# Seven of sixteen layer-0 products as three rounded matmuls, three chunks per tile scaled in PSUM, and another order in the last group

## The chip, the cores and the metric

The kernel runs on one core of one Trainium2 chip. The metric is the device time of one execution in microseconds (us), as a median over runs. Everything is float32, so TensorE works either on float32 operands or on operands rounded to its rounded type (float32r), of which several are needed for one float32 product.

## What is computed

The reference is three layers of a compressed interaction network. Each layer forms, for every batch row and embedding element, all products of a field of the current features with a field of the input, multiplies them by a weight matrix and sums over the embedding.

```python
# input: (512, 64, 16); W0: (128, 64*64); W1, W2: (128, 64*128); b: (128,)
x_vec = input
for W, b in params:
    z = jnp.einsum('bhd,bfd->bhfd', x_vec, input)
    z = z.reshape(B, h * f, d)
    x_vec = jnp.einsum('oc,bcd->bod', W, z) + b[None, :, None]
    outs.append(x_vec.sum(axis=2))
return jnp.concatenate(outs, axis=1)          # (512, 384)
```

## The kernel before

**Tiles and groups.** A column is one (batch row, embedding element) pair. 128 columns (8 batch rows) are a tile, four tiles are a group, and 16 groups cover the batch. TensorE works through the groups one after the other (`groups`, bodies "first", 14 times "inner", "last"), each body in 64 steps `e`: four tiles `j` of 16 chunks `c`, so `e = 16 j + c`.

**Layer 1** is the bulk. A step computes one chunk: `y` (128 columns x 512) by `by_parts` (line 686), which is three rounded matmuls, xh by wh, xh by wl and xl by wh, where h is the rounded upper part of an operand and l the remainder. Four PSUM banks hold chunks, so chunk c+4 waits until chunk c has been read. A chunk holds four fields. Each must be scaled by its column's field value in `x0t` and added up. VectorE does that for 11 of 16 chunks with four instructions each (`add_fields`, lines 617 and 619). ScalarE scales the five HELPED chunks (1, 4, 7, 10, 13) into `prod` (`multiply`, line 525), and GpSimd adds these (lines 369, 371). `combine` on GpSimd (lines 377 to 382) then makes the tile's `x2`.

**Layer 0 of the next group** is made between the chunks. SyncE copies shifted rows of the input `xg` into one of nine slots of `z` (`front`, line 296, two transfers per step `t`), GpSimd multiplies the slot by `xg` (`product`, line 360), and TensorE multiplies by `w0t` in float32 (`layer0`, line 705) at the steps `AHEAD_AT` (9, 11, 14, ... 55 for t = 0 ... 16). A slot is loaded again once its matmul has read it (`z_used`). The last step, t = 16, is one rounded matmul (line 701). In the first group the rest of group 0's own layer 0 (384 columns) runs in steps 0 to 11 (`LATER_AT`), and only then does group 1's begin.

**Layer 2** needs `x2` of the tile before (line 767, at c = 12), and once in four groups, and at the end, 64 float32 matmuls (line 755, `quarter`). In steps 12 to 27 of the first group the 16 pieces of W2 are transposed (line 744) and copied out by ScalarE (`w2_out`, line 482).

**Order.** Every engine runs its own hand-written list in order, with semaphores between. Nothing reorders it. The turn of a group (steps 56 to 63 and 0 to 8) holds no layer-0 matmul, but ScalarE and VectorE split the new layer-0 result there (`upper`, line 463; `fields`, line 450; `lower`, line 594; `sum_elements`, line 601). `own_rows` (line 584) is VectorE's other work, once per tile.

**Before and after the groups.** The prologue pairs and transposes W0 (line 803), computes layer 0 of the first 128 columns in float32 (`early_layer0`, line 727, 16 matmuls) and splits W1 (lines 544 and 673). After the last chunk come `combine` on GpSimd, layer 2 of the last tile, the last quarter, 12 transposes (line 860), four copies and four stores.

## Time and profile before

| what | us |
|---|---|
| three runs | 1128.06, 1128.33, 1129.62 |
| median | 1128.33 |
| the profiled execution's own time | 1127.95 |
| its span, first to last instruction | 1126.2 |
| TensorE busy | 1095.7 (97%) |
| VectorE busy | 868.8 (77%) |
| GpSimd busy | 836.8 (74%) |
| ScalarE busy | 451.4 (40%) |
| mean granted TensorE clock | 0.997 of full |

The profiled execution took 1.75 us more than its span, which lies before and after the instructions, and 0.38 us less than the median. A matmul's end in the trace is modelled and matmuls overlap, so a group's busy time says little of what one costs. What one costs is read from the distance between starts, or from the chain of waits, which counts only the time to the next step. A float32 matmul stands as two records, so "x2" at line 705 is one matmul.

### The profile page before, as it was taken

To read this page: it belongs to the slowest core of one execution; us is meant where nothing else is said; L and a number is where in the kernel's file an instruction comes from. 1 tells how busy PE (TensorE), PEld (TensorE's weight loads), DVE (VectorE), ACT (ScalarE), POOL (GpSimd) and SP (SyncE) were. 2 spreads that over 40 slices of the span, in tenths; PEclk is the share of its full clock that TensorE was granted. 3 is DMA by queue.
4 is the path that set the end of the run, shared out by engine and by line. 5 is a ranking of instruction groups with operands and counts; after the bars stand their busy time and mean duration, and the time that the engine had idled before them with its cause. 6 is when DMAs were issued, how large, how long until landed. Compare 5 with 4: busy or idle time off the path is not lost.

```text
span 1126.2 us, 17047 instructions
## 1 busy us (share of the span) xinstructions
PE 1095.7 (97%) x4690; PEld 786.3 (70%) x4690; DVE 868.8 (77%) x3008; ACT 451.4 (40%) x1533; POOL 836.8 (74%) x765
## 2 busy tenths in 40 slices
PE   5989999999999999999999999999999999999996
PEld 5766667666677667666678666676677776666776
DVE  3556879888884888879794798978887598888990
ACT  1443435343432444434351343534343243434550
POOL 4568887969784697878875788787978479697561
PEclk9999999999999999999999999999999999999998
DMA  7952414223141231405141051423323142240000
GB/s 245 251 114 60 112 54 94 73 56 104 17 122 36 58 102 24 124 27 122 46 103 47 17 122 45 105 62 80 87 42 95 31 94 73 51 109 9 1 1 29
DMA packets 112352, 85.82 MB, mean 76 GB/s; under 512 B 75136, under 2 KB 77920, under 8 KB 112128
## 3 DMA queue, kind: packets, MB, share of 16 engines
q1 hardware_dynamic: 110528, 78.37, 28.9%
q10 hardware_dynamic: 1728, 6.36, 1.5%
q8 instruction: 37, 0.61, 0.2%
q14 instruction: 59, 0.48, 0.1%
HBM read 14.75 MB, written 0.79 MB: 14 GB/s over the span
## 4 chain that ended last, share of the span: by engine, by line
PE 83%; DVE 13%; issue 2%; DMA 1%; ACT 1%; POOL 1%; SPq 0%; POOLq 0%; ACTq 0%
PE y L692 53%; PE l L705 19%; DVE acc L619 8%; PE xt L755 5%; PE l2p L767 3%; DVE bd L584 2%; DVE w1l L673 1%; DVE x1l L594 1%; DMA gram<-in_L_rec_W_dram 1%; PE l2p L744 1%; DMA z<-xg 0%; PE l2p L717 0%; ACT prod L525 0%; PE xt L737 0%; PE l L727 0%
## 5 line engine op out<-in xcount | busy, mean ns | idle before, releaser
L619 DVE SCALAR_TENSOR_TENSOR acc<-y,x0t,acc 128x128 f32<-128x128 f32 x2560 | 698.8, 341 | 206.1 <-PE y L692 204.0
L525 ACT ACTIVATE prod<-y,x0t 128x128 f32<-128x128 f32 x1280 | 366.0, 369 | 610.5 <-PE y L692 578.7
L692 PE MATMUL y<-w1h,x1h 128*128 128x512 f32 x1024 | 509.3, 497 | 6.0 <-DVE acc L619 4.3
L692 PE MATMUL y<-w1h,x1l 128*128 128x512 f32 x1024 | 403.5, 394 | 0.0
L692 PE MATMUL y<-w1l,x1h 128*128 128x512 f32 x1024 | 402.4, 393 | 0.0
L371 POOL TENSOR_TENSOR pacc<-pacc,prod 128x512 f32<-128x512 f32 x192 | 247.4, 1289 | 191.6 <-ACT prod L525 191.6
L360 POOL TENSOR_TENSOR z<-z,xg 128x512 f32<-128x512 f32 (+2 forms) x272 | 348.3, 1288 | 23.7 <-DMA z<-xg 23.7
L692 PEld LDWEIGHTS y<-w1h,x1h 128*128 128x128 f32 x1024 | 192.8, 188 | 132.8 <-issue 59.2
L705 PE MATMUL l<-z,w0t 128*128 128x512 f32 (+1 forms) x512 | 257.5, 585 | 0.6 <-POOL z L360 0.6
L692 PEld LDWEIGHTS y<-w1l,x1h 128*128 128x128 f32 x1024 | 192.8, 188 | 82.2 <-issue 54.1
L692 PEld LDWEIGHTS y<-w1h,x1l 128*128 128x128 f32 x1024 | 192.1, 188 | 43.6
L705 PEld LDWEIGHTS l<-z,w0t 128*128 128x128 f32 x512 | 95.5, 189 | 23.7 <-POOL z L360 1.9
L369 POOL TENSOR_TENSOR pacc<-prod 128x512 f32<-128x512 f32 x64 | 85.4, 1334 | 28.7 <-ACT prod L525 28.7
L377 POOL TENSOR_TENSOR pacc<-pacc,acc 128x512 f32<-128x512 f32 x64 | 83.1, 1298 | 4.0 <-DVE acc L619 3.3
L755 PEld LDWEIGHTS xt<-gram,w2t 128*128 128x128 f32 x512 | 63.0, 197 | 3.6 <-ACT sums L470 1.5
L755 PE MATMUL xt<-gram,w2t 128*128 128x128 f32 x512 | 63.4, 281 | 0.8 <-ACT sums L470 0.8
L584 DVE TENSOR_TENSOR bd<-x0t,own_half 128x256 f32<-128x256 f32 x64 | 62.4, 976 | 0.0
L617 DVE TENSOR_SCALAR acc<-y,x0t 128x128 f32<-128x128 f32 x192 | 54.9, 341 | 0.0
L379 POOL TENSOR_TENSOR pacc<-pacc 128x256 f32<-128x256 f32 x64 | 46.9, 732 | 5.0
L767 PE MATMUL l2p<-bd,x 64*128 64x260 f32 x256 | 45.9, 435 | 4.5 <-POOL x L382 4.5
L468 ACT COPY gram<-l2p 128x512 f32<-128x512 f32 x64 | 38.6, 603 | 5.5 <-PE l2p L767 5.5
L767 PEld LDWEIGHTS l2p<-bd,x 64*128 64x128 f32 x256 | 19.5, 186 | 27.9 <-issue 22.5
(65 smaller groups left out, 300.8 us busy)
## 6 DMA issues: line engine op xcount, KB each, us to landing
z<-xg SPq DMA_DIRECT2D x480, 128.0 KB, 2.4
xg<-in_r_input_dram SPq DMA_DIRECT2D x32, 128.0 KB, 3.9
w2t<-in_L_rec_W_dram ACTq DMA_DIRECT2D x8, 512.0 KB, 7.1
gram<-in_L_rec_W_dram SPq DMA_DIRECT2D x8, 512.0 KB, 5.9
z<-xg SPq DMA_DIRECT2D x32, 96.0 KB, 4.0
z<-xg SPq DMA_DIRECT2D x15, 192.0 KB
gram<-in_L_rec_W_dram ACTq DMA_DIRECT2D x1, 2048.0 KB, 7.9
out_dram<-z SPq DMA_DIRECT2D x4, 192.0 KB, 2.1
```

What stands on the lines that cost most here:

```text
L360: nc.gpsimd.tensor_tensor(z[0:rows, slot, cols], z[0:rows, slot, cols], xg[0:rows, cols], ALU.mult).then_inc(z_made, 1)
L369: nc.gpsimd.tensor_tensor(pacc[:], prod[:, 0], prod[:, 1], ALU.add).then_inc(pool_step, 1)
L371: nc.gpsimd.tensor_tensor(pacc[:], pacc[:], prod[:, h % HSLOTS], ALU.add).then_inc(pool_step, 1)
L377: nc.gpsimd.tensor_tensor(pacc[:], pacc[:], acc[:, slot], ALU.add).then_inc(pool_step, 1)
L525: last = nc.scalar.activation(prod[:, h % HSLOTS, k, :], y[c % YB][:, k * O:(k + 1) * O], ACT.Copy, scale=x0t[:, j, f:f + 1])
L584: nc.vector.tensor_tensor(bd[:, j % 2, 0:GRAM].rearrange("p (b f) -> p b f", f=F), x0t[:, j, :].unsqueeze(1).to_broadcast(shape), own_half ...
L617: ins = nc.vector.tensor_scalar(to, of, x0t[:, j, f:f + 1], None, ALU.mult)
L619: ins = nc.vector.scalar_tensor_tensor(out=to, in0=of, scalar=x0t[:, j, f:f + 1], in1=b1r[:] if m == 0 else to, op0=ALU.mult, op1=ALU.add)
L692: ins = nc.tensor.matmul(to, stationary, moving, start=(first and k == 0), stop=(last and k == 2))
L705: nc.tensor.matmul(l0[:, cols], w0t[:, t, :], z[:, slot, cols], start=(t == 0), stop=False).then_inc(z_used, 1)
L755: last = nc.tensor.matmul(l2, w2t[:, f, :], gram[:, f, :], start=(f == 0), stop=(f == F - 1))
L767: last = nc.tensor.matmul(l2p[:, k, 0:GRAM + HALF_B], x2[half, slot], bd[half, slot, :], start=True, stop=True)
```

## The change

- `PARTED` is the seven odd steps t = 1, 3, ... 13 of layer 0. Their products are split by ScalarE (`part_upper`, a rounding copy of `z` into `zh`) and VectorE (`part_lower`, `z` minus `zh` into `zl`), and TensorE uses `by_parts` on them with split weights `w0h` and `w0l`. Nine steps stay float32. Two slots hold `zh` and `zl`. In the prologue, W0 is split in the same way, and `early_layer0` does each parted step with two float32 matmuls instead of one.
- To make room, `z` has six slots instead of nine. In the first group GpSimd makes 6 products ahead instead of 9. In the others one product moves from step 0 of tile 3 to step 4 of tile 2.
- Chunks 3, 9 and 15 of each tile (3, 9 and 12 in the last group) are scaled in place in PSUM by ScalarE (`scale`, four instructions), and VectorE adds the whole chunk to `acc` with one instruction instead of four.
- In the last group, the first three of four output rows are transposed and copied during the chunks. At the end VectorE combines the last tile in two instructions instead of GpSimd in three. One output row is left for the end.

```diff
-ZSLOTS = 9
+ZSLOTS = 6
+PARTED = tuple(range(1, 15, 2))
+ZHSLOTS = 2
+SCALED = (3, 9, 15)
+SCALED_LAST = (3, 9, 12)
+ROWS_AT = (34, 40, 46)
-LATER_PRODUCTS = (9, (2, 2, 2, 2, 0))
-AHEAD_FIRST_AT = [22 + t * 33 // (ZT - 1) for t in range(ZT)]
+LATER_PRODUCTS = (6, (3, 3, 3, 2, 0))
+AHEAD_FIRST_AT = [24 + t * 31 // (ZT - 1) for t in range(ZT)]
+LATER_PARTED_AT = [{t: LATER_AT[t] - k for t in PARTED} for k in (2, 1)]
+PARTED_AT = [{AHEAD_AT[t] - k: t for t in PARTED} for k in (6, 4)]
-PRODUCTS_AT = ((2, 1, 1, 1, 1), (1, 1, 1, 1, 1), (1, 1, 1, 1, 0), (2, 0, 0, 0, 0))
+PRODUCTS_AT = ((2, 1, 1, 1, 1), (1, 1, 1, 1, 1), (1, 1, 1, 1, 1), (1, 0, 0, 0, 0))
...
+            def part_upper(n, t):
...
+                act.wait_ge(z_made, ZT * n + t + 1)
...
+                nc.scalar.copy(zh[:, i % ZHSLOTS, cols], z[:, zslot(t), cols]).then_inc(zh_made, 1)
...
+            def scale(tile, j, c):
+
+                act.wait_ge(y_made, CHUNKS * tile + c + 1)
+                for k in range(CF):
+                    f = CF * c + k
+                    of = y[c % YB][:, k * O:(k + 1) * O]
+                    last = nc.scalar.activation(of, of, ACT.Copy, scale=x0t[:, j, f:f + 1])
+                last.then_inc(y_scaled, 1)
...
+            def part_lower(n, t):
...
+                dve.wait_ge(zh_made, i + 1)
+                nc.vector.tensor_tensor(zl[:, i % ZHSLOTS, cols], z[:, zslot(t), cols],
+                                        zh[:, i % ZHSLOTS, cols].bitcast(F32), ALU.subtract).then_inc(zl_made, 1)
...
+                if c in scaled_in(tile):
+                    dve.wait_ge(y_scaled, scaled_at(tile, c))
+                    dve.wait_ge(acc_step, added(tile, SUMMED[m - 1]))
+                    to = acc[:, j % 2].rearrange("p k o -> p (k o)")
+                    nc.vector.tensor_tensor(to, y[c % YB][:], to, ALU.add).then_inc(acc_step, 1)
+                    return
...
+                if t in PARTED:
+                    i = PARTED.index(t)
+                    at = (PN * n + i) % ZHSLOTS
+                    pe.wait_ge(zl_made, PN * n + i + 1)
+                    by_parts(l0[:, cols], zh[:, at, cols], zl[:, at, cols], w0h[:, i, :], w0l[:, i, :],
+                             t == 0, False, False).then_inc(z_used, 1)
+                    return
```

The order on **TensorE** at steps 29 to 32 of an inner group. The rows are chunks (`y`) and a layer-0 product into `l`. Before:

```order
L692 MATMUL y<-w1h,x1l 128x512
L705 MATMUL l<-z,w0t 128x512
L692 MATMUL y<-w1h,x1h 128x512
L692 MATMUL y<-w1l,x1h 128x512
L692 MATMUL y<-w1h,x1l 128x512
```

and now:

```order
L817 MATMUL y<-w1h,x1l 128x512
L817 MATMUL l<-zh,w0h 128x512
L817 MATMUL l<-zh,w0l 128x512
L817 MATMUL l<-zl,w0h 128x512
L817 MATMUL y<-w1h,x1h 128x512
```

One float32 matmul has become three rounded ones at the same place.

The order on **ScalarE** at the turn of a group, from the split of the new layer 0 (`x1h`, 384 columns) to the late `x0t`. The rows between are `prod`, the copies of layer 2 and the split of the last 128 columns. Before:

```order
L463 ACTIVATE x1h<-l,b0c 128x384
L450 COPY x0t<-xt 128x192
L525 ACTIVATE prod<-y,x0t 128x128 x8
L468 COPY gram<-l2p 128x64x8
L470 COPY sums<-l2p 128x8
L463 ACTIVATE x1h<-l,b0c 128x128
L525 ACTIVATE prod<-y,x0t 128x128 x8
L450 COPY x0t<-xt 128x64
```

and now:

```order
L527 ACTIVATE x1h<-l,b0c 128x384
L514 COPY x0t<-xt 128x192
L604 ACTIVATE y<-y,x0t 128x128 x4
L615 ACTIVATE prod<-y,x0t 128x128 x8
L532 COPY gram<-l2p 128x64x8
L534 COPY sums<-l2p 128x8
L604 ACTIVATE y<-y,x0t 128x128 x4
L527 ACTIVATE x1h<-l,b0c 128x128
L615 ACTIVATE prod<-y,x0t 128x128 x4
L604 ACTIVATE y<-y,x0t 128x128 x4
L615 ACTIVATE prod<-y,x0t 128x128 x4
L494 CAST zh<-z 128x512
```

Three scalings in PSUM and one rounding copy of `z` have come in between.

The order on **VectorE** after that turn, from the split of the last 128 columns (`x1l`) to `bd` of tile 0. Before:

```order
L594 SCALAR_TENSOR_TENSOR x1l<-l,b0c,x1h 128x128
L619 SCALAR_TENSOR_TENSOR acc<-y,x0t,acc 128x128 x4
L601 TENSOR_REDUCE sums<-l 128x32
L619 SCALAR_TENSOR_TENSOR acc<-y,x0t,acc 128x128 x16
L584 TENSOR_TENSOR bd<-x0t,own_half 128x256
```

and now:

```order
L693 SCALAR_TENSOR_TENSOR x1l<-l,b0c,x1h 128x128
L727 SCALAR_TENSOR_TENSOR acc<-y,x0t,acc 128x128 x4
L700 TENSOR_REDUCE sums<-l 128x32
L727 SCALAR_TENSOR_TENSOR acc<-y,x0t,acc 128x128 x4
L666 TENSOR_TENSOR zl<-z,zh 128x512
L727 SCALAR_TENSOR_TENSOR acc<-y,x0t,acc 128x128 x4
L712 TENSOR_TENSOR acc<-y,acc 128x512
L727 SCALAR_TENSOR_TENSOR acc<-y,x0t,acc 128x128 x4
L683 TENSOR_TENSOR bd<-x0t,own_half 128x256
```

Chunk 9 is now one instruction, and the subtraction of the first parted product stands among the chunks.

## Rows read from the trace of the kernel before

**Rows 1.** The page: busy us, share of the span and instructions per engine.

```profile
PE 1095.7 (97%) x4690; PEld 786.3 (70%) x4690; DVE 868.8 (77%) x3008; ACT 451.4 (40%) x1533; POOL 836.8 (74%) x765
```

**Rows 2.** Windows: length; busy us of PE, PEld, DVE, ACT, POOL; clock, DMA share, GB/s.

```profile
252.40:315.05 62.65, 62.40 (x246) 43.23 (x246) 52.98 (x185) 26.73 (x96) 51.81 (x46) 1.00 0.31 75
315.05:392.20 77.15, 76.90 (x373) 57.49 (x374) 53.28 (x185) 26.99 (x97) 51.81 (x46) 1.00 0.25 60
1047.90:1098.00 50.10, 49.01 (x208) 35.95 (x208) 50.10 (x186) 25.55 (x92) 30.82 (x29) 1.00 0.00 1
```

**Rows 3.** Chain of waits (start, us, what): steps and turn of an inner group.

```profile
266.68 2.09 PE y L692 x9
268.77 0.86 PE l L705 x2
...
309.87 0.12 issue
309.99 0.92 DVE acc L619 x4
```

**Rows 4.** Groups of instructions by form: a VectorE operation on a whole PSUM bank.

```profile
L673 DVE TENSOR_TENSOR w1l<-y,w1h 128x512 fp32r<-128x512 f32 x16 | 9.7, 678 | 4.2 <-ACT w1h L544 4.2
```

**Rows 5.** Tiles bd and zleft: durations in ns, min/median/max, first and last start.

```profile
L584 DVE TENSOR_TENSOR bd<-x0t,own_half x64: 406/1030/1427, 62.3 to 1095.2; 128x256 f32<-128x256 f32 x64
...
L440 ACT CAST zleft<-z x16: 513/620/621, 60.2 to 1036.7; 96x512 fp32r<-96x512 f32 x15, 96x384 fp32r<-96x384 f32 x1
L575 DVE TENSOR_TENSOR zleft<-z,zleft x16: 550/762/772, 60.7 to 1039.0; 32x512 fp32r<-32x512 f32 x15, 32x384 fp32r<-32x384 f32 x1
```

**Rows 6.** Timelines of DVE, ACT and PE at the turn of a group.

```profile
306.92 5.47 DVE L619 SCALAR_TENSOR_TENSOR acc<-y,x0t,acc 128x128 f32<-128x128 f32 x20
...
309.75 0.35 ACT L450 COPY x0t<-xt 128x192 f32<-128x192 f32 x1
...
315.05 0.47 PE L692 MATMUL y<-w1h,x1h 128*128 128x512 f32 x1 [0.24 <-DVE acc L619]
```

**Rows 7.** First group: timelines of SP, POOL and PE; last, a row of DMA issues.

```profile
42.44 2.99 SPq L296 DMA_DIRECT2D z<-xg  x4
...
53.42 0.65 SPq L301 DMA_DIRECT2D z<-xg  x1
...
58.18 1.95 POOL L360 TENSOR_TENSOR z<-z,xg 128x384 f32<-128x384 f32 x2
...
61.31 0.45 PE L701 MATMUL l<-zleft,w0left 96*128 96x384 f32 x1 [0.47 <-DVE zleft L575]
...
z<-xg SPq DMA_DIRECT2D x32, 96.0 KB, 4.0
```

**Rows 8.** Chain of waits: early layer 0, and a W2 step behind ScalarE.

```profile
25.18 4.24 PE l L727 x32
...
63.00 0.71 PE y L692 x3
...
63.74 1.14 ACT prod L525 x4
...
65.41 0.85 PE l2p L744 x4
```

**Rows 9.** Timeline of all engines at the end.

```profile
1099.23 1.43 POOL L377 TENSOR_TENSOR pacc<-pacc,acc 128x512 f32<-128x512 f32 x1 [0.58 <-DVE acc L619]
...
1102.05 1.24 PE L767 MATMUL l2p<-bd,x 64*128 64x260 f32 x4 [4.54 <-POOL x L382]
...
1104.04 16.67 PE L755 MATMUL xt<-gram,w2t 128*128 128x128 f32 x128 [0.75 <-ACT sums L470]
...
1122.31 1.82 SPq L311 DMA_DIRECT2D out_dram<-z  x4
```

**Rows 10.** Windows at the end, columns as in rows 2.

```profile
1100.00:1101.00 1.00, 0.00 (x0) 0.00 (x0) 0.00 (x0) 0.00 (x0) 0.92 (x2) 1.00 0.00 0
...
1102.00:1103.00 1.00, 0.95 (x4) 0.51 (x4) 0.00 (x0) 0.00 (x0) 0.00 (x0) 0.50 0.00 0
```

More of the change, by code:

```diff
@@ L232, in z_rows, with in_last, scaled_in, add_steps @@
             return P if t < ZT - 1 else ZCOPIES * ZLAST
-        def tile_added(tile):
-            return SN * tile + 2 * SN
+        def in_last(tile):
+            return isinstance(tile, int) and tile >= LAST_TILES
+        def scaled_in(tile):
+            return SCALED_LAST if in_last(tile) else SCALED
+        def add_steps(scaled, upto):
+            return sum(1 if c in scaled else CF for c in SUMMED if c <= upto)
+        SN = add_steps(SCALED, CHUNKS)
+        def added_before(tile):
+            if in_last(tile):
+                return SN * LAST_TILES + SN + add_steps(SCALED_LAST, CHUNKS) * (tile - LAST_TILES)
+            return SN * tile + SN
+        def added(tile, c):
+            return added_before(tile) + add_steps(scaled_in(tile), c)
+        def tile_added(tile):
+            return added_before(tile + 1)
+        def scaled_at(tile, c):
+            before = len(SCALED) * tile
+            if in_last(tile):
+                before = len(SCALED) * LAST_TILES + len(SCALED_LAST) * (tile - LAST_TILES)
+            return before + scaled_in(tile).index(c) + 1
         def x2_ready(tile):
@@ L506, in body @@
                             quarter_out(n // QG)
+                    if kind == "first":
+                        for t in PARTED:
+                            if LATER_PARTED_AT[0][t] == e and LATER_PARTED_AT[0][t] >= 0:
+                                part_upper(0, t)
+                        if e in PARTED_FIRST_AT[0]:
+                            part_upper(1, PARTED_FIRST_AT[0][e])
+                    if kind == "inner" and e in PARTED_AT[0]:
+                        part_upper(n + 1, PARTED_AT[0][e])
                     if kind == "first" and e == LATER_LEFT_PARTS_AT:
@@ L538, in _ @@
                 act.wait_ge(prep_made, turned_in(PREP[:k]) + 1)
-                if not parted(what, r):
-                    nc.scalar.copy(w0t[:, 4 * r:4 * r + 4, :],
-                                   y[bank][:].rearrange("p (t o) -> p t o", o=O)).then_inc(y_used[bank], 1)
-                    continue
+                if what == "w0" and r < W0_STEPS - 1:
+                    for t in range(4 * r, 4 * r + 4):
+                        if t in WHOLE:
+                            nc.scalar.copy(w0t[:, WHOLE.index(t), :], y[bank][:, t % 4 * O:(t % 4 + 1) * O])
                 part, of = weights(w1h, what, r, bank, slice(0, z_rows(ZT - 1)))
@@ L549, in _ @@
             quarter_out(QUARTERS)
-            for r in range(0, B // P, 2):
-                act.wait_ge(turned, r + 1)
-                nc.scalar.copy(outs[:, r, :], y[r][:, 0:L * O]).then_inc(outs_made[0], 1)
+            row_out(B // P - 1)
         @block.vector
@@ L637, in body @@
                         own_rows(n * TILES + j, j)
+                    if kind == "first":
+                        for t in PARTED:
+                            if LATER_PARTED_AT[1][t] == e and LATER_PARTED_AT[0][t] >= 0:
+                                part_lower(0, t)
+                        if e in PARTED_FIRST_AT[1]:
+                            part_lower(1, PARTED_FIRST_AT[1][e])
+                    if kind == "inner" and e in PARTED_AT[1]:
+                        part_lower(n + 1, PARTED_AT[1][e])
                     if kind == "first" and e == LATER_LEFT_LOWER_AT:
@@ L777, in chunk @@
                 else:
-                    value = SN * tile + (SN + CF * SUMMED.index(before) + CF) - (SN if late else 0)
-                    pe.wait_ge(acc_step, value)
+                    pe.wait_ge(acc_step, added(tile - 1 if late else tile, before))
                 cols = slice(j * P, (j + 1) * P)
```

105 lines of the change are left out of this document (80 added, 25 removed).

## Prediction

> **What bounds the kernel now.** I read the busy shares first, then windows cut at group starts, then the chain of waits inside one inner group, and last the stages that aren't groups. TensorE is busy 97% of the span, VectorE 77%, GpSimd 74% [rows 1]. Within an inner group it is tighter: TensorE is busy 62.4 of 62.65 us, VectorE 53.0, GpSimd 51.8, ScalarE 26.7 [rows 2]. The chain of such a group is TensorE nearly throughout: nine matmuls of three chunks take 2.09 us, or 0.232 each, and one float32 product into `l` 0.86 [rows 3]. So TensorE's work sets the groups, and what it is spared counts almost fully. There are two exceptions. At the turn of a group, about 6 us with no layer-0 matmul, chunks come faster than VectorE reads them, and the first chunk of a group waits for VectorE [rows 6]. The last group is one long turn: VectorE is busy for all of 50.1 us, TensorE for 49.0 [rows 2].
>
> **1. Three rounded matmuls for one.** Each costs 3 x 0.232 = 0.695 us in place of 0.86, so 0.165 less [rows 3]. Seven steps for each of groups 1 to 15 make 105, and 105 x 0.165 = **-17.3 us**. Bounds: 0.155 per step (16.3 us) to 0.19 (20 us), since a period of nine matmuls and one product repeats within 0.02 us through the group. The same steps of group 0, with 384 columns, are left at nothing: smaller matmuls leave little between the two forms.
>
> **2. What VectorE and ScalarE take on.** ScalarE gets 12 scalings of four instructions (1.14 each [rows 8]) and seven copies (0.62, by the nearest, zleft [rows 5]) per group: 26.7 + 13.7 + 4.3 = 45 of some 61 us, which fits. VectorE gives up 12 chunks of 0.92 + 0.12 = 1.04 us [rows 3] for 12 whole-bank additions at about 0.6 to 0.68 [rows 4] plus the same 0.12 wait, a saving of 0.3 each, 3.6 in all. It takes on seven subtractions with both inputs in SBUF. Their price isn't in the trace. `zleft`, such an operation on 32 partitions, takes 0.76, and `bd`, also with both inputs in SBUF, takes 0.41 to 1.43 with a median of 1.03 for half the columns [rows 5]: it varies with what GpSimd does at that moment. So 0.68 to 1.95, and I take 0.68 + (1.03 - 0.41) = 1.3, because GpSimd is busy 83% of the group. That is 9.1 us. VectorE comes to 53.0 - 3.6 + 9.1 = 58.5 of about 61.5 us. It still fits, but no longer loosely, so I follow one turn.
>
> The Trainium skill, GPSIMD Engine Reference, section 1 (Specifications), says that GpSimd shares its SBUF interfaces with VectorE and that VectorE instructions with two SBUF inputs contend with it. The spread of bd, 406 to 1427 ns, agrees [rows 5]. The rule speaks against this change, which adds 105 such instructions to groups where GpSimd has little idle time. Without it, by the 0.76 of zleft alone, the turns would cost nothing and the sum would be 1113; at its worst it gives the second rival.
>
> The turn after 308 us: ScalarE is busy with x1h and `x0t` until 310.10 [rows 6], so chunk 9 is scaled by 310.1 + 1.1 = 311.2 and added by 311.8. Before, VectorE had added it at 309.2 + 2 x 1.04 = 311.3. It idles for 0.9 us before a shorter instruction, and everything behind it (chunk 11, `bd`, `x1l`, chunk 12) is 0.5 late. The group's first chunk waits for chunk 12 [rows 6], so it starts 0.5 later. About 0.2 comes back, since the following chunks had waited 0.2 before. Next, VectorE ran about 1 us behind around chunk 8 of tile 0. The first subtraction, 1.3 less 0.3, uses that up: another 0.1. Then each layer-0 step gives slack again. Sum **+0.4 per turn**, 15 turns, **+6 us**. Bounds: 0 (the skipped work helps as much as it hurts) to 1.0 (longer subtractions), so 0 to 15 us.
>
> The Trainium skill, ScalarE: Activation LUTs, section Step-by-step, says that ScalarE writes faster to PSUM than to SBUF. No row here shows such a write. By it the scaling would take under 1.14 us, and the 0.5 of the turn would be smaller.
>
> **3. GpSimd and the six slots, inner groups.** With nine slots a product's transfer waits for the matmul nine steps before, now for the one six steps before. Six steps are about 17 us, against two issues of 0.6, some 2.4 to 4 of landing [rows 7] and 1.3 of product. Nothing ends late there, and the product moved up a slot lets `xg` load 1.3 us sooner. Each rounding copy waits on ScalarE for its product, with multiplications queued behind, but the products end before the place of the copy, or up to 1 us into idle time of ScalarE. Cost 0.
>
> **4. Prologue and first group.** Early layer 0 is 16 matmuls in 4.24 us [rows 8], 0.265 each. Seven more cost 1.9, and the split of W0 ahead of them some 0.7: +2.6 before the first chunk. Then the slots bite. Before, SyncE waited at 42.44 for the first matmul on a slot and had t = 9 to 16 left, until 53.42 + 0.65 = 54.07 [rows 7]. Now it waits at the same event, 2.6 later, with t = 6 to 16 left: ten pairs of 1.24, five pieces of W2 of 0.63 and one single of 0.65 make 16.2 us, to 61.2. The last transfer lands 4.0 later [rows 7], then come product, rounding copy and subtraction (1.0 + 0.55 + 0.55): 67.4, against 61.31 before. So **+6.1** at step 11, the 2.6 included (5 to 7.5). In steps 12 to 27 a W2 step waits for ScalarE after a multiplied chunk: behind the chunk at 63.00 come a W2 step and another chunk, so the next W2 step could start at 63.00 + 0.7 + 0.5 + 0.6 = 64.8 and starts at 65.41, a stall of 0.6, four times [rows 8]. Chunks 15, 19 and 25 are now scaled by ScalarE too: 0.6 + 0.5 + 0.5 = **+1.6** (0.5 to 3). Together +7.7 (5.5 to 10.5).
>
> **5. Last group and end.** VectorE sets 12.1 us per tile in the last group. Three whole-bank additions take 0.9 off, and TensorE's own 64 chunks of 0.69 with four layer-2 steps and 9 transposes of the output come to 47.9 us. But each scaled chunk passes two engines (1.14 + 0.6 + waits = 2.0) while its bank is wanted back after three chunks, 2.07, so I expect 0.3 of the 0.9 per tile to be lost again, and the transposes eat most of the rest: **-0.5** (-2 to +1.5). `combine` and its wait took 1099.2 to 1102.05, 2.85 us [rows 9]. Two VectorE instructions at 0.7 take 1.45: **-1.4**. The output's last part took 1126.2 - 1120.7 = 5.5 us with 12 transposes, copies and four issues of 0.45 [rows 9]. With a quarter of each, 4.3: **-1.2**. And the clock: TensorE had been idle for 4.54 us up to 1102.05 [rows 9]; the granted clock was full at 1100 to 1101 and half at 1102 to 1103 [rows 10], that is at its 1.2 GHz level. The last quarter then took 16.67 us [rows 9], where the same matmuls cost 77.15 - 62.65 = 14.5 in an inner group [rows 2], and layer 2 took 1.24 instead of about 0.65. With `combine` 1.4 shorter TensorE idles 3.1 us, and I take it that the clock stays: **-2.7** (or 0). End: -5.8 with the last group.
>
> **Sum.** -17.3 + 6 + 7.7 - 5.8 = -9.4. The profiled execution took 1127.95, so 1118.6, and the median is 0.38 above that execution: **1119 us**, 0.8% faster.
>
> **Rivals.**
> - *No price at the turns* (0.23). Subtractions near 0.7 us and quick scaling: turns 0, first group 5.5, last group -1. That is -17.3 + 5.5 - 6.3 = -18, so 1110. For it: VectorE idles before most chunks away from the turn. Against: it doesn't idle at the turn.
> - *The ports* (0.14, slower). If each subtraction takes 1.95 and holds GpSimd up besides, VectorE's 58.5 becomes 63 us per group, more than TensorE's 61.5. Then each group gives back about 1.8 instead of 0.4: +27 instead of +6, 1140 at the far end. It is slower than before from 1.0 us per group on (9.4 / 15 more than 0.4). For it: the maximum of bd. Against: its median.
> - *Rounded steps don't gain as said* (0.07). If a switch between forms has a price of its own and a step saves 0.08, the gain is 8.4 and the time 1128: no change. Against: the single rounded matmul at line 701 runs at chunk pace.
> - *The clock still falls, and the first group costs 10* (0.14): 1119 + 2.7 + 2.3 = 1124.
>
> **Chances.** The forecast has 0.42. A measurement of this kernel tells about 0.2% (2.3 us) from no change. Faster takes the forecast, the first and the last rival, and a bit of the others, 0.79. The same has 0.08, slower 0.13. The range goes from the first rival's time to just short of the slower ones: 1109 to 1129.
>
> **What would show it.** Right: 0.69 to 0.70 us on the chain for three matmuls into `l`; inner groups of 61.6 to 62.1 us; the first left step (96 x 384) near 67.4; the last quarter near 14.5 at full clock; about 4.3 us behind it. Wrong: waits for `zl` in front of TensorE in every group, a subtraction near 1.9 us, GpSimd's products ending after their copies' places, or a scaled chunk far from 1.14 us.

## The result and the profile after

| | before | after |
|---|---|---|
| median of 11 runs, us | 1128.3 | 1125.21 |
| lowest to highest, us | 1126.84 to 1129.62 | 1123.52 to 1126.48 |
| profiled span, us | 1126.2 | 1123.5 |

The ratio is 0.9973 with an interval of 0.9965 to 0.9981: faster by 0.3%, where 0.8% was forecast. The direction was right, the size a third of the forecast. The following tables of stages are made from the starts of the same instruction in each trace: the first chunk, the left step of group 0 (96 x 384), layer 2 at e = 28, the left step of group 1 (e = 55, 96 x 512), that of group 15, layer 2 at e = 60 of the last group, layer 2 of the last tile, the transposes of the output and the end.

| stretch, us | before | after | difference | forecast |
|---|---|---|---|---|
| start to first chunk | 40.81 | 41.87 | +1.06 | +2.6 |
| to the left step of group 0 | 20.50 | 27.94 | +7.44 | +3.5 |
| to e = 28 (W2 steps) | 26.75 | 28.46 | +1.71 | +1.6 |
| to e = 55 of the first group | 32.00 | 36.35 | +4.35 | -1.2 |
| 14 groups, e = 55 to e = 55 | 920.89 | 904.78 | -16.11 | -10.5 |
| to e = 60 of the last group | 53.57 | 55.44 | +1.87 | -0.1 |
| to layer 2 of the last tile | 7.53 | 6.40 | -1.13 | -1.4 |
| layer 2 and last quarter | 19.20 | 18.93 | -0.27 | -2.7 |
| output | 4.95 | 3.33 | -1.62 | -1.2 |
| sum | | | -2.7 | -9.4 |

The groups gave more than forecast, and everything but them gave less. The page's busy line, which answers [rows 1], shows TensorE 18 us less busy with 126 more matmul records, GpSimd 36 us busier, and VectorE no busier.

```profile
PE 1077.4 (96%) x4816; PEld 808.6 (72%) x4816; DVE 859.1 (76%) x2548; ACT 709.8 (63%) x2424; POOL 872.4 (78%) x762
```

Windows of the changed kernel, in the columns of [rows 2]: an inner group, the last group, and two single microseconds at the end, which answer [rows 10].

```profile
196.10:257.62 61.52, 60.80 (x254) 44.58 (x253) 51.84 (x157) 42.82 (x148) 54.64 (x46) 1.00 0.32 77
...
1047.90:1098.00 50.10, 48.85 (x214) 36.02 (x212) 45.68 (x144) 38.71 (x140) 29.57 (x28) 1.00 0.04 13
...
1100.00:1101.00 1.00, 0.00 (x0) 0.00 (x0) 0.97 (x2) 0.00 (x0) 0.00 (x0) 0.69 0.00 0
1102.00:1103.00 1.00, 0.47 (x4) 0.00 (x0) 0.00 (x0) 0.48 (x1) 0.00 (x0) 0.50 0.00 0
```

VectorE has 51.8 us of work in a group, against a forecast of 58.5. The clock column (third from the end) reads 0.69 and then 0.50, the 1.2 GHz level: it fell again.

The subtractions and the rounding that feed them, by their tile (ns, min/median/max):

```profile
L666 DVE TENSOR_TENSOR zl<-z,zh x112: 545/736/2462, 41.7 to 1027.6; 128x512 fp32r<-128x512 f32 x105, 128x384 fp32r<-128x384 f32 x7
```

The median is 0.74 us, near the forecast's lower bound, but single ones take up to 2.46. The minimum is of the 384-column form; of the 512-column ones, the eight that no GpSimd instruction overlaps take 0.68.

The timeline of the first group (start, us, engine, idle time before in brackets). First t = 7 of group 0, then its end, then t = 11 and 13 of group 1, last the turn of a later group:

```profile
34.62 11.02 SPq L351 DMA_DIRECT2D z<-xg  x4
...
52.34 0.51 ACT L494 CAST zh<-z 128x384 fp32r<-128x384 f32 x1 [4.45 <-POOL z L415]
52.76 1.11 ACT L604 ACTIVATE y<-y,x0t 128x128 f32<-128x128 f32 x4
53.90 0.69 DVE L712 TENSOR_TENSOR acc<-y,acc 128x512 f32<-128x512 f32 x1 [4.61 <-ACT y L604]
54.51 0.55 DVE L666 TENSOR_TENSOR zl<-z,zh 128x384 fp32r<-128x384 f32 x1
55.11 0.45 PE L817 MATMUL l<-zh,w0h 128*128 128x384 f32 x1 [3.62 <-DVE zl L666]
...
69.81 0.44 PE L826 MATMUL l<-zleft,w0left 96*128 96x384 f32 x1 [0.46 <-DVE zleft L674]
...
121.31 0.50 PE L817 MATMUL l<-zh,w0h 128*128 128x512 f32 x1 [0.95 <-DVE zl L666]
123.61 2.51 POOL L415 TENSOR_TENSOR z<-z,xg 128x512 f32<-128x512 f32 x2
125.44 2.46 DVE L666 TENSOR_TENSOR zl<-z,zh 128x512 fp32r<-128x512 f32 x1
127.95 0.50 PE L817 MATMUL l<-zh,w0h 128*128 128x512 f32 x1 [2.06 <-DVE zl L666]
...
402.64 0.47 PE L817 MATMUL y<-w1h,x1h 128*128 128x512 f32 x1 [0.72 <-DVE acc L727]
```

Three things are to be seen. SyncE's four issues take 11.02 us where four take 2.4 (2.99 in [rows 7], the first after a wait), so 8.6 us are a wait for a slot. At t = 7 four engines stand in a row: product, rounding copy, a scaled chunk and its addition, subtraction, and TensorE waits 3.62 us for the last. And at 125.44 a subtraction takes 2.46 us beside a GpSimd product and the first two instructions of `combine`, and TensorE waits 2.06 for it.

A fourth thing is in the granted clock (columns as in [rows 2]; two windows of the changed kernel, then one of the kernel before):

```profile
43.00:45.00 2.00, 2.00 (x6) 1.35 (x5) 1.59 (x5) 0.00 (x0) 0.00 (x0) 0.50 0.03 8
56.00:59.00 3.00, 3.00 (x7) 2.00 (x6) 1.59 (x5) 0.51 (x1) 1.57 (x2) 0.50 1.01 260
...
41.00:130.00 89.00, 85.86 (x350) 60.28 (x349) 56.37 (x190) 36.59 (x112) 62.54 (x56) 1.00 0.51 121
```

From 42.2 to 45.7 and from 55.9 to 59.3 us the changed kernel ran at the 1.2 GHz level with TensorE busy throughout. The kernel before kept the full clock through its first group. The second fall comes just after the wait of 3.62 us. Ahead of the first one TensorE had waited 1.54 us, but the kernel before waits 1.53 there and kept its clock, so the rows don't say why it fell. Half the clock over these 6.8 us costs at most 3.4 us (an estimate from their lengths). The executions differ by it: over the 11 of the changed kernel the mean granted clock goes from 0.992 to 0.997 of full, and the two at 0.992 took 1126.1 and 1126.5 us, the two at 0.997 1123.5 and 1123.8.

The end of the changed kernel, same view, answering [rows 9]:

```profile
1099.44 0.69 DVE L800 TENSOR_TENSOR acc<-acc,pacc 128x512 f32<-128x512 f32 x1
1100.16 1.02 DVE L803 TENSOR_REDUCE x<-acc 128x128 f32<-128x512 f32 x1
1101.24 1.24 PE L916 MATMUL l2p<-bd,x 64*128 64x260 f32 x4 [3.41 <-DVE x L803]
1103.23 16.44 PE L904 MATMUL xt<-gram,w2t 128*128 128x128 f32 x128 [0.75 <-ACT sums L534]
1120.17 0.52 PE L886 MATMUL l<-ident,sums 128*128 128x128 f32 x3 [0.51 <-issue]
```

### The profile page after: what moved, and what is told of

Same layout as the page of the kernel before. It is cut to its first block, busy times and chain, and to the rows that moved or that the text cites. A ratio compares the mean times of both kernels' runs of the same rounds, so it can differ in the third digit from the quotient of the medians.

```text
span 1123.5 us, 17841 instructions
## 1 busy us (share of the span) xinstructions
PE 1077.4 (96%) x4816; PEld 808.6 (72%) x4816; DVE 859.1 (76%) x2548; ACT 709.8 (63%) x2424; POOL 872.4 (78%) x762
## 4 chain that ended last, share of the span: by engine, by line
PE 87%; DVE 7%; ACT 2%; DMA 2%; issue 1%; POOL 0%; SPq 0%; ACTq 0%; DVEq 0%
PE y L817 59%; PE l L837 10%; PE l L817 6%; PE xt L904 5%; DVE acc L727 3%; PE l2p L916 3%; DVE bd L683 1%; DMA z<-xg 1%; DVE w1l L792 1%; DVE x1l L693 1%; DMA gram<-in_L_rec_W_dram 1%; PE l2p L893 1%; ACT y L604 1%; DVE zl L666 1%; ACT prod L615 0%
## 5 line engine op out<-in xcount | busy, mean ns | idle before, releaser
L727 DVE SCALAR_TENSOR_TENSOR acc<-y,x0t,acc 128x128 f32<-128x128 f32 x1792 | 493.8, 341 | 78.2 <-PE y L817 72.7
L817 PE MATMUL y<-w1h,x1h 128*128 128x512 f32 x1024 | 467.4, 456 | 13.4 <-DVE acc L727 11.8
L415 POOL TENSOR_TENSOR z<-z,xg 128x512 f32<-128x512 f32 (+2 forms) x272 | 373.4, 1377 | 31.6 <-DMA z<-xg 31.6
L604 ACT ACTIVATE y<-y,x0t 128x128 f32<-128x128 f32 x768 | 215.1, 349 | 79.7 <-PE y L817 79.5
L712 DVE TENSOR_TENSOR acc<-y,acc 128x512 f32<-128x512 f32 x192 | 132.6, 691 | 139.1 <-ACT y L604 135.7
L837 PE MATMUL l<-z,w0t 128*128 128x512 f32 (+1 forms) x288 | 146.4, 590 | 0.0
L666 DVE TENSOR_TENSOR zl<-z,zh 128x512 fp32r<-128x512 f32 (+1 forms) x112 | 95.2, 850 | 0.3 <-ACT zh L494 0.3
L494 ACT CAST zh<-z 128x512 fp32r<-128x512 f32 (+1 forms) x112 | 70.5, 631 | 34.3 <-POOL z L415 33.9
L837 PEld LDWEIGHTS l<-z,w0t 128*128 128x128 f32 x288 | 54.3, 190 | 11.6 <-POOL z L415 0.4
L817 PE MATMUL l<-zh,w0h 128*128 128x512 f32 (+1 forms) x112 | 45.2, 404 | 9.6 <-DVE zl L666 9.6
```

What stands on the lines that cost most here:

```text
L415: nc.gpsimd.tensor_tensor(z[0:rows, slot, cols], z[0:rows, slot, cols], xg[0:rows, cols], ALU.mult).then_inc(z_made, 1)
L604: last = nc.scalar.activation(of, of, ACT.Copy, scale=x0t[:, j, f:f + 1])
L666: nc.vector.tensor_tensor(zl[:, i % ZHSLOTS, cols], z[:, zslot(t), cols], zh[:, i % ZHSLOTS, cols].bitcast(F32), ALU.subtract).then_inc(zl ...
L712: nc.vector.tensor_tensor(to, y[c % YB][:], to, ALU.add).then_inc(acc_step, 1)
L727: ins = nc.vector.scalar_tensor_tensor(out=to, in0=of, scalar=x0t[:, j, f:f + 1], in1=b1r[:] if m == 0 else to, op0=ALU.mult, op1=ALU.add)
L817: ins = nc.tensor.matmul(to, stationary, moving, start=(first and k == 0), stop=(last and k == 2))
```

## The experiments

The questions were: what the first group lost, and how much of it is the slots, the splitting and the scaling; whether the scaled chunks and VectorE's work set the inner groups; and what made the clock fall. Ratios are to the kernel before, in the same runs. The stretches are those of the table above. Each row is one profiled execution. The run with every subtraction done twice, which has the changed kernel's code up to the left step, took 25.85 us there and not 27.94, and the first chunk of the changed kernels comes anywhere from 41.87 to 43.10. So 1 or 2 us in the first two columns, in one row, aren't yet an effect of the edit.

| us | to first chunk | to left step | to e = 28 | to e = 55 | 14 groups | to e = 60 | layer 2, quarter |
|---|---|---|---|---|---|---|---|
| before | 40.81 | 20.50 | 26.75 | 32.00 | 920.89 | 53.57 | 19.20 |
| after | 41.87 | 27.94 | 28.46 | 36.35 | 904.78 | 55.44 | 18.93 |
| six slots alone | 39.93 | 26.42 | 27.45 | 31.72 | 920.92 | 53.52 | 18.62 |
| no scaling | 42.25 | 27.91 | 27.30 | 35.64 | 901.46 | 54.54 | 18.64 |
| earlier split | 42.37 | 28.02 | 30.00 | 31.65 | 905.01 | 55.49 | 18.78 |
| busy end | 42.07 | 28.10 | 28.36 | 36.37 | 904.99 | 55.46 | 16.53 |
| subtraction twice | 42.05 | 25.85 | 28.45 | 37.95 | 991.87 | 55.53 | 19.34 |
| W2 early | 43.03 | 23.06 | 28.37 | 36.34 | 904.75 | 55.51 | 18.08 |
| eight parted | 42.13 | 27.97 | 27.18 | 37.01 | 915.62 | 55.31 | 18.65 |
| four together | 42.76 | 22.51 | 27.17 | 30.92 | 901.47 | 54.63 | 16.52 |
| scaled mid tiles | 43.10 | 27.84 | 27.67 | 38.00 | 901.59 | 55.81 | 18.62 |
| before, two edits | 40.30 | 26.34 | 26.75 | 32.08 | 920.72 | 53.56 | 16.57 |
| eight and mid tiles | 42.17 | 22.25 | 27.19 | 30.73 | 916.03 | 55.30 | 16.53 |

**Six slots alone**, on the kernel before:

```diff
-ZSLOTS = 9
+ZSLOTS = 6
-LATER_PRODUCTS = (9, (2, 2, 2, 2, 0))
+LATER_PRODUCTS = (6, (3, 3, 3, 2, 0))
-AHEAD_FIRST_AT = [22 + t * 33 // (ZT - 1) for t in range(ZT)]
+AHEAD_FIRST_AT = [24 + t * 31 // (ZT - 1) for t in range(ZT)]
```

(and `PRODUCTS_AT` as in the change)

> The kernel before with one part of the change alone: six slots of z in place of nine, GpSimd's six products ahead and the later places of group 1's layer-0 steps that go with them. Theory 1 (the slots are a good part of what the first group lost): SyncE waits at 42.44 us as before, but with t = 6 to 16 still to issue, 16.2 us, so the last single lands near 62.6 and the left step (96 x 384) starts near 64.8 instead of 61.31; up to e = 56 of the first group 3 to 4 us more than the 120.29 of before, inner groups still 62.65, time near 1131.5. Rival (the loss comes from the splitting of products alone): left step before 62.3, time 1128 to 1129.

Measured: 1134.18 us, 1.0052 (1.0037 to 1.0067). Theory 1, and more than it: the left step comes 5.9 us later after the first chunk, not 3.5, and inner groups are unchanged to 0.03 us in 14. SyncE's queue took the 16.2 us of the forecast, but the forecast let the last transfer meet an idle GpSimd. The timeline shows it wasn't idle:

```profile
57.65 0.67 SPq L301 DMA_DIRECT2D z<-xg  x1
...
60.05 1.96 POOL L360 TENSOR_TENSOR z<-z,xg 128x384 f32<-128x384 f32 x2 [0.43 <-DMA z<-xg]
...
63.22 1.95 POOL L360 TENSOR_TENSOR z<-z,xg 128x384 f32<-128x384 f32 x2
...
66.35 0.44 PE L701 MATMUL l<-zleft,w0left 96*128 96x384 f32 x1 [0.47 <-DVE zleft L575]
```

From the last issue's end (58.3) to the left step are 8.0 us, where the forecast had 6.1: the last four products go one behind another, with an addition of GpSimd among them. Here the clock was full in the first group, so the loss isn't the clock's.

**No scaling**, on the changed kernel:

```diff
-SCALED = (3, 9, 15)
-SCALED_LAST = (3, 9, 12)
+SCALED = ()
+SCALED_LAST = ()
```

> The changed kernel with no chunk scaled in PSUM: VectorE takes all eleven chunks in four instructions again; all else is as changed. Theory 1 (scaling helps the inner groups and hurts the first): the wait of 3.62 us at t = 7 gets 1.6 shorter, since the subtraction no longer stands behind a chunk that ScalarE has yet to scale; the W2 steps gain 1.7; up to e = 56 of the first group about 130.5 instead of 134.86. In inner groups VectorE has 3.6 us more to do, about 59 of 61.5, and a group takes 61.9, so 14 x 0.4 = 5.6 more; time near 1126. Rival (scaling is of no use anywhere): inner groups of 61.2, since the turn loses its 0.3, and a time near 1117. Second rival (VectorE becomes the bound without it): inner groups over 62.5, time 1135 or more.

Measured: 1120.34 us, 0.9933 (0.9916 to 0.9949), 4.9 us below the changed kernel. In the groups the first rival is right: 61.27 in place of 61.50. In the first group theory 1 is right about the W2 steps (1.2 of 1.7) and wrong about t = 7, where the left step didn't move. The window of an inner group and the wait at the turn:

```profile
258.00:319.27 61.27, 61.02 (x254) 44.52 (x253) 58.84 (x192) 30.43 (x100) 54.86 (x46) 1.00 0.32 77
```

```profile
399.73 0.47 PE L817 MATMUL y<-w1h,x1h 128*128 128x512 f32 x1 [0.24 <-DVE acc L727]
```

VectorE is busy 58.84 us, by chance nearly what the forecast had for the changed kernel (58.5), and TensorE doesn't wait for it more than before: 0.24 us at the turn as in [rows 6]. So scaling takes 7 us of work from VectorE per group, nobody needs them there, and TensorE pays 0.23 for them. The subtraction's median is 1.21 us here, not 0.74: its price depends on where it stands.

**Earlier split**, on the changed kernel:

```diff
-PARTED_FIRST_AT = [{AHEAD_FIRST_AT[t] - k: t for t in PARTED} for k in (4, 2)]
+PARTED_FIRST_AT = [{AHEAD_FIRST_AT[t] - k: t for t in PARTED} for k in (6, 4)]
```

> The changed kernel with one table changed: in the first group, group 1's products are copied and subtracted 6 and 4 steps ahead of their matmuls, as in the inner groups, not 4 and 2. Theory 1 (TensorE waits in steps 28 to 56 because the subtraction stands too close to its matmul and takes 1.7 to 2.5 us beside a GpSimd product): the waits of 1.29, 0.27, 0.95 and 2.06 us go, steps 28 to 56 take 32.2 us instead of 36.5, time 1121. Rival (what counts is VectorE's work in that stretch, wherever it stands): the waits return in front of chunks, a gain below 1 us, time 1124.5. Second rival (the copies now stand ahead of GpSimd's products and hold ScalarE): no gain or up to 2 us lost.

Measured: 1122.55 us, 0.9947 (0.9933 to 0.9962). Theory 1 for steps 28 to 55: 4.7 us less, no wait for `zl` left there. The second rival takes 1.5 back in the W2 steps: rounding copies now stand ahead of their products on ScalarE, and a W2 copy is behind them. A late one, and one of the few waits of TensorE that remain:

```profile
122.76 0.62 ACT L494 CAST zh<-z 128x512 fp32r<-128x512 f32 x1 [2.91 <-POOL z L415]
...
124.48 0.50 PE L817 MATMUL y<-w1h,x1h 128*128 128x512 f32 x1 [0.32 <-ACT prod L615]
```

**Busy end**, on the changed kernel (the added matmuls compute nothing that is used):

```diff
             groups(pe, body)
+            pe.wait_ge(outs_made, len(ROWS_AT))
+            for k in range(13):
+                nc.tensor.matmul(l0[:], w1h[:, 0, 0:P], w1h[:, k, :], start=True, stop=True)
             layer2(GROUPS * TILES - 1, 1)
```

> The changed kernel with 13 more rounded matmuls on TensorE behind the last chunk, into a bank that nobody reads, while VectorE combines the last tile (3.41 us of idle time of TensorE). They add work and compute nothing that is used. Theory 1 (the granted clock fell to half because TensorE had nothing to do there): the clock stays full, the last layer-2 step takes 0.65 instead of 1.24 us and the last quarter 14.5 instead of 16.44, time 2.5 us less, 1122.7. Rival (the clock falls there for another reason): half clock from 1101 as before, time 1125 to 1126.

Measured: 1123.75 us, 0.9959 (0.9945 to 0.9974). Theory 1: the timeline has layer 2 at 0.71 us, not 1.24, and the quarter at 14.56, not 16.44.

```profile
1098.16 3.11 PE L1003 MATMUL l<-w1h 128*128 128x512 f32 x13
...
1101.77 0.71 PE L916 MATMUL l2p<-bd,x 64*128 64x260 f32 x4 [0.50 <-DVE x L803]
...
1103.23 14.56 PE L904 MATMUL xt<-gram,w2t 128*128 128x128 f32 x128 [0.75 <-ACT sums L534]
```

So the clock fell at the end because TensorE had nothing to do for 3.41 us. By the trace that is 2.4 us for layer 2 and the quarter (18.93 against 16.53). The medians differ by 1.5, since the first group varies between executions: in this profiled one the clock was low from 52.0 to 58.9 us.

**W2 early**, on the changed kernel:

```diff
-                    if first and t % 2 == 0 and t // 2 < W_PARTS:
-                        part = slice(t // 2 * F * O // W_PARTS, (t // 2 + 1) * F * O // W_PARTS)
+                    for k in {0: (0,), 2: (1,), 4: (2,), 5: (3, 4, 5, 6, 7)}.get(t, ()) if first else ():
+                        part = slice(k * F * O // W_PARTS, (k + 1) * F * O // W_PARTS)
```

> The changed kernel with five DMA issues in another place: the pieces 3 to 7 of W2 go out right behind the two transfers of t = 5, while SyncE has nothing to do but wait for a slot (34.62 to 44.45 us), not behind t = 6, 8, ... 14. Theory 1 (with six slots SyncE's queue and the transfers behind it set the left step): 5 x 0.63 = 3.1 us leave the stretch between the first chunk and the left step, 27.94 in the changed kernel, about 24.8 here; waits at t = 7 and 9 shorter; time 1122. Rival (the splitting sets it: product, copy, scaled chunk, subtraction): the left step comes at most 1 us sooner, time 1124.5. Second rival (the pieces take the transfer engines from t = 6 and 7): the first waits grow and nothing is won.

Measured: 1122.25 us, 0.995 (0.9935 to 0.9965). Theory 1: the left step comes 4.9 us sooner after the first chunk. By the medians (1122.25 against 1125.21) the edit is worth 3.0, the 3.1 of issuing. The profiled execution was the fastest of its four, and its clock didn't fall in the first group; how much of the 4.9 is due to that wasn't separated. What is left of the waits for `zl` is 0.44, 1.58, 0.97 and 0.67 us, at most. SyncE's row, with the five issues in the idle time and the rest without a stop:

```profile
36.39 3.06 SPq L359 DMA_DIRECT2D gram<-in_L_rec_W_dram  x5
44.67 14.27 SPq L351 DMA_DIRECT2D z<-xg  x20
```

**Every inner subtraction twice**, on the changed kernel:

```diff
                 dve.wait_ge(zh_made, i + 1)
+                if n > 1:
+                    nc.vector.tensor_tensor(zl[:, i % ZHSLOTS, cols], z[:, zslot(t), cols],
+                                            zh[:, i % ZHSLOTS, cols].bitcast(F32), ALU.subtract).then_inc(once, 1)
+                    dve.wait_ge(once, i - 2 * PN + 1)
```

> The changed kernel with every subtraction of groups 2 to 15 done twice, one behind the other with a wait between, so that a parted step costs VectorE some 1.5 us: what the forecast took as its price, and a little more. Theory 1 (VectorE has room at 51.8 of 61.5 us, and the price of a subtraction is nothing to TensorE as long as it ends before its matmul): inner groups 61.5 to 61.6, time 1125 to 1127. Rival (the forecast's account, in which each group's turn grows with that price): 0.3 to 0.5 more per group, time 1130 to 1132. Second rival (two SBUF inputs each, GpSimd is held up too): inner groups over 62.5, time 1140.

Measured: 1212.36 us, 1.0744 (1.0726 to 1.0762), beyond every expectation: inner groups take 68.2 us. The window and the two instructions by their tile:

```profile
300.00:368.20 68.20, 64.38 (x265) 44.45 (x264) 63.75 (x162) 41.44 (x144) 56.21 (x46) 1.00 0.29 69
```

```profile
L671 DVE TENSOR_TENSOR zl<-z,zh x112: 547/1655/2482, 41.9 to 1114.6; 128x512 fp32r<-128x512 f32 x105, 128x384 fp32r<-128x384 f32 x7
...
L668 DVE TENSOR_TENSOR zl<-z,zh x98: 681/877/1702, 149.4 to 1113.8; 128x512 fp32r<-128x512 f32 x98
```

The pair takes 0.88 + 1.66 = 2.5 us by the medians, not 1.5. VectorE's work comes to 63.75, more than the 61.5 that TensorE needs, so VectorE alone makes the group longer, with 4.5 us of its own waits on top (the added semaphore wait between the two is part of the edit). This wasn't the test that it was meant to be, since it added 12 us, not 5. It shows that the forecast's slower rival exists once VectorE has 12 us more work per group. Where between 0 and 12 it begins isn't shown.

**Eight parted steps**, on the kernel without scaling:

```diff
-PARTED = tuple(range(1, 15, 2))
+PARTED = tuple(range(1, 16, 2))
```

> The changed kernel with no scaled chunk (as in the run without scaling, where inner groups took 61.27) and with step 15 parted as well, eight steps in place of seven. Theory 1 (a parted step saves 0.20 us in a group, whatever VectorE does): inner groups 61.07, first group the same within 0.5, time 1117.5. Rival (VectorE, at 58.8 of 61.3 busy without scaling, is about full): the eighth subtraction makes it 60.0, and groups get longer, over 61.5, time 1124 or more. Second rival (step 15's copy and subtraction stand close to those of step 16 and to the turn): 61.2 to 61.4.

Measured: 1135.23 us, 1.0067 (1.0052 to 1.0082). Inner groups take 62.33, the rival. VectorE's work is 60.72:

```profile
391.00:453.30 62.30, 61.52 (x254) 44.44 (x253) 60.72 (x193) 30.96 (x101) 54.97 (x46) 1.00 0.32 76
```

By this alone one would say that VectorE is full at about 60 us. The last run contradicts that.

**Four together**: no scaling, W2 early and the busy end as above, and copies and subtractions of group 1 in the first group 5 and 3 steps ahead.

```diff
-PARTED_FIRST_AT = [{AHEAD_FIRST_AT[t] - k: t for t in PARTED} for k in (4, 2)]
+PARTED_FIRST_AT = [{AHEAD_FIRST_AT[t] - k: t for t in PARTED} for k in (5, 3)]
```

> The changed kernel with four of the edits together: no scaled chunk, W2's pieces in SyncE's idle time, group 1's copies and subtractions 5 and 3 steps ahead of their matmuls in place of 4 and 2, and 13 rounded matmuls into an unused bank that keep TensorE busy at the end. Theory 1 (four separate losses that add up): from 1120.3 without scaling, 3.1 for SyncE, 2.5 to 3.5 for the waits in steps 28 to 56, 2.4 for the clock at the end: 1111 to 1112.5. Rival (the first group's losses overlap, and what one edit frees another wait takes): 1115 to 1117.

Measured: 1107.73 us, 0.9823 (0.9808 to 0.9838), 20.6 us below the kernel before and 17.5 below the changed one. Theory 1's losses are separate, and together they come to more than it said (1111). Part of the excess can be the clock: it stayed full in this trace's first group, and over the four executions its mean was 0.998 to 1.000, against 0.992 to 0.997 in the changed kernel. That share wasn't separated. From the first chunk to e = 55 it takes 80.6 us, where the kernel before took 79.25 and the changed one 92.75.

**Scaled in the second and third tile only**, on the changed kernel (`SCALED_LAST` goes with it):

```diff
+def SCALED_HERE(n, j):
+    return SCALED if j in (1, 2) else ()
...
         def scaled_in(tile):
 
-            return SCALED_LAST if in_last(tile) else SCALED
+            n, j = divmod(tile, TILES)
+            return SCALED_HERE(n, j)
```

(the counts of additions follow from it)

> The changed kernel with chunks scaled in PSUM in the second and third tile of each group only, so none near the turn and none before step 16 of the first group. Theory 1 (the price of scaling is paid at the turn alone, where ScalarE is busy with the new x1h and x0t when chunk 9 comes): TensorE's wait there is 0.24 us as before, not 0.72, and inner groups take 61.27, as with no scaling at all, though six chunks are still scaled; time near 1121.5. Rival (each scaled chunk costs a little wherever it stands): 61.38, half way between 61.27 and 61.50, time near 1123.

Measured: 1123.07 us, 0.9955 (0.9938 to 0.9971). For the inner groups theory 1: 14 of them take 901.59, as without scaling (901.46), and the wait at the turn is 0.25. The time is above the expected 1121.5. In the profiled execution, the slowest of the four at 1124.21, the first group's last part took 38.0 us, 1.65 more than in the changed kernel. The clock accounts for it. The waits for `zl` are those of the changed kernel (1.31, 0.30, 0.97 and 2.07 against 1.29, 0.27, 0.95 and 2.06), and then the clock is at its lower level for 3.4 us of TensorE's work. The same window of this run and of the changed kernel:

```profile
130.00:133.00 3.00, 3.00 (x7) 1.68 (x6) 2.63 (x9) 0.00 (x0) 0.00 (x0) 0.50 0.44 59
...
130.00:133.00 3.00, 3.00 (x13) 1.97 (x11) 2.23 (x6) 2.22 (x8) 0.00 (x0) 1.00 0.46 73
```

TensorE gets through 7 matmul records at half the clock where it got through 13. The run with the doubled subtraction (37.95 against 36.35) and the eight parted steps (37.01 against 35.64 without scaling) have the same fall at 127 us, also just behind the wait of 2.06 us.

**The kernel before with two edits**: W2's pieces 4 to 7 behind t = 8 of nine slots, and the busy end with 18 matmuls.

```diff
-                    if first and t % 2 == 0 and t // 2 < W_PARTS:
+                    for k in {0: (0,), 2: (1,), 4: (2,), 6: (3,), 8: (4, 5, 6, 7)}.get(t, ()) if first else ():
...
             groups(pe, body)
+            pe.wait_ge(l0_used, GROUPS)
+            for k in range(18):
+                nc.tensor.matmul(l0[:], w1h[:, 0, 0:P], w1h[:, k % CHUNKS, :], start=True, stop=True)
```

> The kernel before, with nine slots and nothing parted or scaled, and two of the edits: W2's pieces 4 to 7 issued behind t = 8, while SyncE waits for a slot, and 18 rounded matmuls into an unused bank at the end, where TensorE has nothing to do for 4.54 us. Theory 1 (both losses were there before the change, the clock's in full, SyncE's in a smaller form): the quarter 14.5 instead of 16.67 and layer 2 0.6 shorter, 2.6 us, and the left step about 1 us sooner than 20.5 after the first chunk; time 1124.5 to 1126. Rival for the first group (with nine slots SyncE is not what sets the left step): only the end moves, 1125.7. If this came near 1108, the gain of the four edits together would have nothing to do with the change.

Measured: 1128.95 us, 1.0011 (1.0001 to 1.0022). The end gained 2.6 as expected. The first group lost 5.8 in the profiled execution, which no expectation had. That execution took 1130.62 us. By the medians (1128.95 against 1128.05) the loss is about 3.5, since the end gained 2.6. The timeline:

```profile
39.87 2.07 SPq L304 DMA_DIRECT2D gram<-in_L_rec_W_dram  x4
...
55.28 2.90 POOL L360 TENSOR_TENSOR z<-z,xg 128x384 f32<-128x384 f32 x3 [8.43 <-DMA z<-xg]
56.33 1.65 PE L705 MATMUL l<-z,w0t 128*128 128x384 f32 x2 [5.07 <-POOL z L360]
```

With nine slots SyncE had only about 2.9 us to wait (in the kernel before, from 40.09 us to the end of [rows 7]'s four issues at 45.43, less the 2.4 that four take), so the four pieces went out right ahead of the transfers of t = 9 and later. GpSimd waits 8.43 us for a transfer, one that came behind four pieces of 0.5 MB. By the medians the same move wins 3.0 us where SyncE waits 8.6 us and loses 3.5 where it waits 2.9.

**Eight parted, scaling in the middle tiles**, on the four together:

```diff
-PARTED = tuple(range(1, 15, 2))
+PARTED = tuple(range(1, 16, 2))
+def SCALED_HERE(n, j):
+    return (3, 9, 15) if j in (1, 2) and 0 < n < GROUPS - 1 else ()
...
         def scaled_in(tile):
 
-            return SCALED_LAST if in_last(tile) else SCALED
+            n, j = divmod(tile, TILES)
+            return SCALED_HERE(n, j)
```

(the counts of additions follow from it)

> The kernel with the four edits together (1107.7) with step 15 parted as well, eight in place of seven, and chunks 3, 9 and 15 scaled in the second and third tile of the inner groups only, to give VectorE back the time of the eighth subtraction. Theory 1 (a parted step is worth 0.20 us as long as VectorE stays below about 59 of 61 us): VectorE 57 to 58, inner groups 61.07, time 1105. Rival (the eighth step's copy and subtraction collide with those of step 16, which the eight without scaling showed as a wait of 0.43 us for zleft): 61.3 to 61.5 and a time of 1108 to 1111.

Measured: 1122.42 us, 0.9956 (0.9942 to 0.9971). Inner groups take 62.35, as the eight without scaling, and not the 61.07 expected. The window, and the chain of waits ahead of the turn:

```profile
391.00:453.30 62.30, 61.59 (x254) 44.43 (x254) 56.12 (x175) 37.11 (x125) 54.70 (x46) 1.00 0.32 76
```

```profile
443.50 0.88 DVE zl L665
...
446.48 1.44 DVE zleft L673
```

VectorE has 4.6 us less work here than in the run with 60.72, and the group is as long. So its total doesn't decide. Both runs have the same fourth tile, with the eighth subtraction just ahead of step 16's and of the turn, and there the chain now runs over VectorE. The one more instruction, 1.35 us long in the run of eight and 0.88 here, costs 1.07 us per group and the 0.2 not gained, while with seven (run without scaling) TensorE waits for VectorE no more than before. That it is the place, and not the eighth copy on ScalarE, is read from the chain; moving the step wasn't tried.

## Why the forecast was right in direction and wrong in size

**Step 1 (three rounded matmuls, -17.3).** Right, a little small. On the chain of the changed kernel a parted step takes 0.68 to 0.69, as computed, and nine chunk matmuls behind one take 2.04, not the 2.09 behind a float32 product. By the run without scaling seven steps save 1.39 to 1.41 us per group (62.67 to 61.27), 0.20 each and not 0.165: 14 groups give 19.4.

**Step 2 (turn of a group, +6).** The mechanism was right for one term and wrong for the others. The wait of the first chunk grew from 0.24 to 0.72, the 0.5 that was worked out from ScalarE's queue, and with what comes back a group pays 0.23 (61.50 against 61.27), not 0.4. The subtraction was priced at 1.3 us and measured at 0.74 (1.21 without scaling, near the price taken), and VectorE's work came to 51.8 and not 58.5. But that price wasn't what mattered: with VectorE at 58.84 the groups were shorter still. The scaling, which the forecast took for the help against the subtractions, is the whole price of the turn, and it is paid by the chunks near it alone.

**Step 3 (slots in inner groups, 0).** Right: 920.92 against 920.89.

**Step 4 (prologue and first group, +7.7).** This is the step that failed: +14.56, where +7.7 and a gain of 1.2 from the rounded steps were forecast. It let TensorE wait for nothing behind step 11 but the W2 steps, and let the last transfer meet idle engines. Its four terms, the first of them smaller than said:

- Prologue +1.06, not +2.6. Early layer 0 takes 5.16 us with 23 matmuls in the trace, 0.9 more than with 16, where 1.9 was said.
- Slots: +5.9 to the left step, not +3.5. The forecast followed SyncE's queue and then let one product and one copy follow; GpSimd's own queue stood in between. The changed kernel took 1.5 more than that (27.94 against 26.42), but the same code took 25.85 in another execution, so a price of the splitting here isn't shown. Nor is one of the clock: with the clock low for 3.4 us ahead of the left step that run took 25.85 and the one scaled in the middle tiles 27.84, with 6.8 us the others without W2 early took 27.91 to 28.10.
- W2 steps +1.7, forecast 1.6; without scaling 1.2 of them go.
- Steps 28 to 55: priced at nothing and a gain of 1.2; measured +4.35. The forecast priced the subtraction for inner groups and didn't ask where it stands in the first one: two steps ahead of its matmul instead of four, and beside GpSimd's products in pairs. Moving it by two steps gave 4.7 back in that stretch, of which 1.5 went again in the W2 steps. The clock was full in it, in the changed kernel and in the moved one.

**Step 5 (last group and end, -5.8).** -1.15. The last group took +1.87, not -0.1: nine transposes between chunks take about 1.0 on the chain, and scaling, which was to save 0.9 per tile, costs 0.9 in all (55.44 against 54.54). VectorE, which set that group before, is busy 45.7 of 50.1 us in it and no longer does. `combine` and the output came out as said (-1.13 for -1.4, -1.62 for -1.2). The clock fell all the same, after 3.41 us of idle time where 3.1 was reckoned and taken to be short enough, so 2.4 of the 2.7 stayed away; the run with the busy end has them.

**The rivals.** The last one (clock falls, first group dearer, 1124) was the closest and had its two causes right, though it sized the first group at 10. That its time came out near is luck in part: the groups gave 5.6 more than forecast, and the first group cost 5.8 more than its 10 less the gain of 1.2. The rival of no price at the turns was right on the subtractions; the four together, at 1107.7, come near its 1110, but by edits that it didn't have. The ports are real: the subtraction of 512 columns takes 0.68 us alone and up to 2.46 beside GpSimd, the pair in the doubled run 2.5, and GpSimd's products lengthen beside it (two in 3.15 us instead of 2.5). The Trainium skill, GPSIMD Engine Reference, section 1 (Specifications), says that such VectorE instructions contend with GpSimd, and the rows agree. But an instruction that is long costs only where someone waits for it.

The Trainium skill, ScalarE: Activation LUTs, section Step-by-step, says that ScalarE writes faster to PSUM than to SBUF. The rows agree, barely: four scalings in place take 1.11 us and four into `prod` 1.14.

**What stays open.** Why a float32 product slows the chunk matmuls behind it (2.09 against 2.04); what makes the stretch to the left step differ by 2 us between executions of the same code; why the clock fell at 42 us after a wait of 1.54 us, and at 127 to 130 us in three runs but not in the changed kernel, which has the same waits; and how much of the gain of the four together is the clock's.

## What to carry to other kernels

Cost an edit in each stage apart: the stretch to step 55 of the first group lost 14.6 us of the 19.4 that the parted steps gave in the others, and all but 3.3 of it came back without scaling and with instructions put elsewhere in their queues, in executions whose clock also stayed up. Ask of a helper engine not how busy it is, but how far ahead of its reader each instruction stands and what is queued before it; VectorE at 58.8 of 61.3 us cost nothing, and one instruction of about 1 us ahead of the turn cost 1 us. And undo a relief that comes with an edit before believing in it: here the scaled chunks cost 4.9 us and relieved nobody.
